# First-layer attention scores: one unit per head on two row halves of TensorE, instead of one unit per two batch rows on the whole array

## The reference, cut to what matters

```python
q = (q_in @ wq + bq).reshape(Bq, Sq, H, DK).transpose(0, 2, 1, 3)   # H = 16, DK = 64
k = (k_in @ wk + bk).reshape(...); v = (v_in @ wv + bv).reshape(...)
scores = einsum('bhqd,bhkd->bhqk', q, k)
scores = where(mask, scores, NEG_INF)          # causal in "sa", padding in both
attn = nan_to_num(softmax(scores / sqrt(DK), axis=-1))
out = einsum('bhqk,bhkd->bhqd', attn, v)...reshape(...) @ wo + bo
```

## Time and profile before

| what | value |
|---|---|
| median of three runs | 2354.99 us |
| the profiled execution | 2356.81 us |
| its span | 2355.1 us |
| granted TensorE clock, mean | 0.964 of full |
| PE busy | 2094.1 us (89%) |
| DVE busy | 1398.9 us (59%) |
| ACT busy | 1138.5 us (48%) |
| POOL busy | 243.7 us (10%) |
| DMA | 8 GB/s over the span |

### The profile page before, as it was taken

How to read it: one execution, slowest core, us unless ns; L and a number is a source line. 1 busy time by engine, 2 the same in 40 slices (tenths; PEclk the granted TensorE clock), 3 DMA queues, 4 the chain that set the end, 5 groups by cost and what they waited for, 6 DMA issues and landing times.

```text
span 2355.1 us, 34008 instructions
## 1 busy us (share of the span) xinstructions
PE 2094.1 (89%) x12584; PEld 1433.4 (61%) x12584; DVE 1398.9 (59%) x3674; ACT 1138.5 (48%) x3857; POOL 243.7 (10%) x271
## 2 busy tenths in 40 slices
PE   5877998899898988999898988999898988897799
PEld 2555666657665666656665666656665666654455
DVE  4544658666675658566675568567675668524410
ACT  3453736456362736456363736456463736331222
POOL 1001011010101011010101011010101011001100
PEclk9989999999999999999999899999999999989999
DMA  5000000000000000000000000000000000000001
GB/s 177 1 1 15 1 1 1 1 15 1 1 1 15 1 1 1 1 15 1 1 1 16 1 1 1 1 16 1 1 1 5 1 1 1 1 1 1 1 10 27
DMA packets 25129, 20.00 MB, mean 8 GB/s; under 512 B 2243, under 2 KB 22790, under 8 KB 24966
## 3 DMA queue, kind: packets, MB, share of 16 engines
q1 hardware_dynamic: 24966, 17.83, 2.6%
HBM read 15.73 MB, written 2.10 MB: 8 GB/s over the span
## 4 chain that ended last, share of the span: by engine, by line
PE 63%; DVE 21%; ACT 11%; issue 4%; POOL 1%; SPq 1%; DMA 0%; POOLq 0%; DVEq 0%
PE ps L655 15%; PE ps L663 9%; PE ps L700 7%; PE ps L798 5%; ACT s_probs L1032 4%; PE ps L785 3%; PE ps L640 3%; PE ps L651 3%; PE ps L813 3%; PE ps L725 3%; ACT probs L1032 3%; DVE keys L1278 3%; DVE stats L1198 2%; DVE probs L1234 2%; DVE tok L1211 2%
## 5 line engine op out<-in xcount | busy, mean ns | idle before, releaser
L1032 ACT ACTIVATE probs<-ps,neg_max 128x128 f32<-128x128 f32 x1024 | 364.9, 378 | 337.1 <-DVE neg_max L1191 336.9
L700 PE MATMUL ps<-keys,queries 128*128 128x256 f32 x1024 | 285.6, 404 | 25.9 <-ACT queries L1026 25.9
L1032 ACT ACTIVATE s_probs<-ps,s_max 128x128 f32<-128x128 f32 x768 | 209.1, 392 | 101.4 <-DVE s_max L1191 100.8
L1191 DVE TENSOR_REDUCE neg_max<-ps 128x4 f32<-128x512 f32 x256 | 176.4, 689 | 129.2 <-PE ps L703 128.0
L700 PEld LDWEIGHTS ps<-keys,queries 128*128 128x128 f32 x1024 | 185.2, 199 | 61.6 <-ACT queries L1026 33.0
L1032 ACT ACTIVATION_READ_ACCUMULATOR probs<-ps,neg_max 128x1 f32 x1024 | 220.6, 216 | 0.0
L1198 DVE BATCH_NORM_STATS2 stats<-ps 128x6 f32<-128x128 f32 x352 | 78.4, 286 | 236.6 <-PE ps L663 229.8
L546 POOL TENSOR_TENSOR rstd<-var_eps,minus_half 128x4 f32<-128x4 f32 x88 | 94.3, 1072 | 1153.3 <-DVE var_eps L1204 1153.3
L1026 ACT ACTIVATE probsT<-ps 128x512 f32<-128x512 f32 x256 | 158.3, 618 | 36.7 <-PE ps L711 35.2
L1191 DVE TENSOR_REDUCE s_max<-ps 128x4 f32<-128x512 f32 x192 | 123.7, 686 | 83.4 <-PE ps L785 82.9
L711 PE MATMUL ps<-ident,probs 128*128 128x128 f32 x1024 | 160.4, 280 | 6.0 <-DVE probs L1234 3.6
(11 more groups left out here) (208 smaller groups left out, 3723.1 us busy)
## 6 DMA issues: line engine op xcount, KB each, us to landing
x_in<-in_x SPq DMA_DIRECT2D x8, 256.0 KB, 3.6
c_in<-in_ctx SPq DMA_DIRECT2D x8, 256.0 KB, 3.8
skip_in<-in_mask_BxS_ik SPq DMA_DIRECT2D x8, 256.0 KB, 3.8
out<-headsT SPq DMA_DIRECT2D x28, 64.0 KB, 1.8
valid_in<-in_mask_BxS_bf SPq DMA_DIRECT2D x8, 64.0 KB, 3.5
w_qkv_sa<-in_L_xattn_sa_wq SPq DMA_DIRECT2D x1, 512.0 KB
w_qkv_sa<-in_L_xattn_sa_wk SPq DMA_DIRECT2D x1, 512.0 KB
w_qkv_sa<-in_L_xattn_sa_wv SPq DMA_DIRECT2D x1, 512.0 KB
```

Source lines behind the costliest of these rows:

```text
L700: mm(bank(MAIN, item)[:, n * 256:n * 256 + 256], queries[:, c % 2, at], keys[:, c % 2, :, at], start=(n == 0), stop=False, skip_group_chec ...
L1032: last = A(dst[:, u % dst.shape[1], h * 128:h * 128 + 128], bank(st, (tag, "s", u))[:, h * 128:h * 128 + 128], ACT.Exp, bias=src_max[:, u ...
L1191: V.tensor_reduce(dst[:, u % 2, :], bank(st, (tag, "s", u)).rearrange("p (h k) -> p h k", h=4), AX.X, ALU.max, negate=True).then_inc(max_r ...
```

## The change

`scores` works on a whole chunk when it comes to the even unit. Unit 2c is now head 0 of all four sequences, and unit 2c + 1 is head 1. TensorE first multiplies the mask into both banks (two 512-column bf16 matmuls), and then runs eight score matmuls of 128 columns that use 64 rows of the array each: rows 0 to 63 for head 0 into one bank, rows 64 to 127 for head 1 into the other, alternately. `keys` holds one version, so it is copied out by one instruction of 128 partitions, and the zeroing at the start goes. `main_steps` puts `s(s)` and `s(s+1)` into the even step; the other items keep their order. A step that held nothing but the odd `s` ("ca", s = 15) is no longer there, so that the list has 115 steps instead of 116. `scale_probs` now has two scalars per tile, and is four `tensor_scalar` instructions of 128 columns where it was two `scalar_tensor_tensor` of 256. `probs` has four slots instead of three. The diff, cut to its core:

```diff
@@ main_steps, attention
-            first = [(tag, "s", s)] if s < UNITS else []
+            first = [(tag, "s", s), (tag, "s", s + 1)] if s < UNITS and s % 2 == 0 else []
...
-        keys = sb("keys", [128, 2, 2, GT])
+        keys = sb("keys", [128, 2, GT])
...
-        probs = sb("probs", [128, 3, 512])
+        probs = sb("probs", [128, 4, 512])
...
-            link(P.memset(keys[64:128, :, 0, :], 0.0))
-            link(P.memset(keys[0:64, :, 1, :], 0.0))
@@ scores
-                c, b0 = u // 2, 2 * (u % 2)
-                before_filling(i, item, (tag, "k", c), (tag, "q", c))
-                for n in range(2):
-                    at = slice((b0 + n) * T, (b0 + n) * T + T)
-                    mm(bank(MAIN, item)[:, n * 256:n * 256 + 256], queries[:, c % 2, at], keys[:, c % 2, :, at],
-                       start=(n == 0), stop=False, skip_group_check=True)
-                mask = (mask_sa if tag == "sa" else mask_ca)[:, b0:b0 + 2, :]
-                mm(bank(MAIN, item), ident_h[:, :], mask.unsqueeze(2).broadcast_to([128, 2, 2, T]),
-                   start=False, stop=True, skip_group_check=True).then_inc(filled[MAIN], 1)
+                if u % 2:
+                    return
+                c = u // 2
+                before_filling(i, item)
+                before_filling(i, (tag, "s", u + 1), (tag, "k", c), (tag, "q", c))
+                mask = (mask_sa if tag == "sa" else mask_ca)[:, :, :]
+                for h in range(2):
+                    mm(bank(MAIN, (tag, "s", u + h)), ident_h[:, :], mask, start=True, stop=False, skip_group_check=True)
+                for b in range(G):
+                    for h in range(2):
+                        rows_of = slice(64 * h, 64 * h + 64)
+                        last = mm(bank(MAIN, (tag, "s", u + h))[:, b * T:b * T + T], queries[rows_of, c % 2, b * T:b * T + T],
+                                  keys[rows_of, c % 2, b * T:b * T + T], start=False, stop=(b == G - 1), skip_group_check=True)
+                        if b == G - 1:
+                            last.then_inc(filled[MAIN], 1)
@@ outputs: which probsT unit and columns
-                    u, n = 2 * c + b // 2, b % 2
                     for h in range(2):
+                        u = 2 * c + h
...
-                                  probsT[:, u % PT, (2 * n + h) * 128:(2 * n + h) * 128 + 128], start=True, stop=True)
+                                  probsT[:, u % PT, b * T:b * T + T], start=True, stop=True)
@@ ScalarE, kind "k" (VectorE likewise)
-                            for h in range(2):
-                                rows_of = slice(64 * h, 64 * h + 64)
-                                last = A(keys[rows_of, c % 2, h, :], bank(MAIN, item)[rows_of, :], ACT.Identity,
-                                         bias=cols[f"L0_xattn_{tag}_bk"][rows_of, c:c + 1], scale=1.0)
-                            last.then_inc(emptied[MAIN, "A"], 1)
+                            A(keys[:, c % 2, :], bank(MAIN, item), ACT.Identity,
+                              bias=cols[f"L0_xattn_{tag}_bk"][:, c:c + 1], scale=1.0).then_inc(emptied[MAIN, "A"], 1)
@@ scale_probs
-                for n in range(2):
-                    p = probs[:, u % 3, n * 256:n * 256 + 256].rearrange("p (h k) -> p h k", h=2)
-                    last = V.scalar_tensor_tensor(out=p, in0=p, scalar=row_ok[tag][:, b0 + n:b0 + n + 1],
-                                                  in1=inv[:, u % 3, 2 * n:2 * n + 2].unsqueeze(2).broadcast_to([128, 2, T]),
-                                                  op0=ALU.mult, op1=ALU.mult)
+                for b in range(G):
+                    p = probs[:, u % 4, b * T:b * T + T]
+                    last = V.tensor_scalar(p, p, inv[:, u % 3, b:b + 1], row_ok[tag][:, b:b + 1], ALU.mult, ALU.mult)
```

10 lines of the change are left out of this document (3 added, 7 removed).

## The result

The changed kernel takes 2446.83 us, median of four runs (2438.45 to 2451.42), beside 2353.64 for the kernel before on the same chip: ratio 1.0391, 95% interval 1.0369 to 1.0413, slower. The forecast was 2391, in a range of 2315 to 2440. The direction was right, the size was not: +93 us instead of +36.

What follows compares the result with a forecast made beforehand. PE, busy 89%, looked like the bound, but waits for ScalarE and VectorE would decide. Seven groups x (6.1 - 0.6) = 38.5 us, first group -3, gave +36: 2355 becomes 2391 us, range 2315 to 2440.

Steps and rivals of the forecast that it cites:

- Scores on PE: Score matmuls of a pair: halves run side by side, 2.15 to 1.70 us, gaining 58 us of PE work over 128 pairs.
- The forecast fall of PE's busy time by 50 us: Whole span, a sign to check: PE's busy time falls by some 50 us while its idle time grows by 85.
- Keys' copy: Copying keys out of PSUM: one instruction instead of two, ScalarE 1.37 to about 0.68 us, VectorE 2 x 0.75 to 0.75.
- Scaling: scale_probs on VectorE: four instructions take 1.3 us a unit against 0.9, 100 us more in all, mostly hidden.
- The ring in the first group: Pairs without side stream: 7.65 us becomes 8.5 (keys by ScalarE) or 6.65 (keys by VectorE), -3 us for the group.
- a sign of being wrong: First group against later groups: the forecast is wrong if the first group loses as much as the others.
- Cross-attention: Eight pairs beside L2: copies and normalised tiles come later behind both units' exponentials and maxima, +6.1 us a group.
- s = 2: Cross-attention pair where the block's layer norm comes later: 11.45 us against 9.0, +2.5.
- Self-attention: Eight pairs beside L1: PE's gain is given back to ScalarE's queue, -0.6 us a group.
- The rest of a group and the end: Layer norms, FFN and the end of each group keep their work: counted as nothing.
- Waits of PE, to grow for ScalarE and for the normalised tiles: PE's waits for keys, kx, s_probs and VectorE's normalised tiles grow, most in cross-attention.
- The clock: PE's granted clock: more standing can lower it, one hundredth costing up to 23 us; named for the range above 2391.

Runs made afterwards that it cites:

- e3: Kernel before with scaling as four tensor_scalar of 128 columns instead of two instructions of 256: 2371.84 us, ratio 1.0059.
- e5: Changed kernel plus six unused matmuls ahead of query projections of chunks 2, 4 and 6 (62 us of added PE work): 2429.85 us, ratio 1.0327.
- e1: Changed kernel, but VectorE and ScalarE take the second unit's maxima and exponentials at their old place, in the odd step: 2397.37 us, ratio 1.0182.
- e16: e11 measured again, unchanged: 2347.73 us, ratio 0.9979 to the kernel before.
- e9: e1 with each mask multiplied twice, 55 us of added PE work inside the scores: 2417.20 us, ratio 1.0210.
- e11: e1 with scaling as a 128x4 product and one product over 512 columns instead of four tensor_scalar: 2350.88 us, ratio 0.9919.
- e12: Changed kernel with scaling as a 128x4 product and one product over 512 columns instead of four tensor_scalar: 2434.20 us, ratio 1.0354.
- e10: Kernel before, whole array, with TensorE filling both units in the even step and maxima and exponentials left in place: 2442.47 us, ratio 1.0315.
- e19: Kernel before with the key projection ahead of the scores in the even step on all engines: 2382.21 us, ratio 1.0126.
- e21: Kernel before plus six unused matmuls ahead of query projections of chunks 2, 4 and 6 (62 us of PE work): 2401.62 us, ratio 1.0198.
- e7: Changed kernel, but ScalarE and VectorE handle the keys' copy between the two units' maxima and exponentials: 2448.28 us, ratio 1.0349.

## Why the prediction was wrong, step by step

- **Scores on PE, 2.15 to 1.70 us a pair.** Right, a little better: 1.61. The Trainium skill, "TensorEngine Tiling (Array Packing)", Key Properties, says that tiles work in parallel and that a change of tiling drains the engine; this trace agrees: the scores take 1.61 us where the halves one by one would have taken 2.17 and more, and the two masks take 0.52 where 2 x 0.215 would be 0.43, the same 0.09 as the forecast read off. The forecast fall of PE's busy time by 50 us didn't show (2094 to 2112 us), since the work ran at a lower clock; at full clock it is there. I had offered it as a test without seeing that. (The projection at 73.87 takes 1.12 us and not 1.13, which changes nothing.)
- **Keys' copy.** Right: 0.72 and 0.74 us.
- **Scaling, 1.3 us a unit.** Too high: 1.11 (four instructions of 0.34, 0.28 apart), so some 60 us more on VectorE and not 100. e3 prices it at 0.6% in the kernel before.
- **The ring in the first group.** Right at full clock for its pairs: 8.5 forecast and 8.54 (e5) for ScalarE's keys, 6.65 and 6.51 (67.25 - 60.74 in e5) for VectorE's. The group's gain of 3 us did not come: by span times clock it is there (205.29 x 0.96 = 197 against 192), but PE stood for 7 us more, and with the clock of 0.89 the group lost 10.6. It lost as much as the later groups, which the forecast had named as a sign of being wrong.
- **Cross-attention, +6.1 us a group.** Right: +6.5, at the same clock. For s = 2 the transposition of the normalised tile was forecast 5.85 us into the pair and the queries 7.35:

```profile
1204.77 0.59 PE L701 MATMUL ps<-mask_ca,ident_h 128*128 128x512 bf16 x2
1205.29 1.16 PE L705 MATMUL ps<-keys,queries 64*128 64x128 f32 x16
...
1210.24 0.66 PE L649 MATMUL ps<-ident,tok 128*128 128x128 f32 x4 [1.75 <-DVE tok L1212]
1211.88 1.84 PE L653 MATMUL ps<-xT_b,w_qkv_ca 128*128 128x512 f32 x2 [0.98 <-ACT keys L1059]
1213.51 1.91 PE L653 MATMUL ps<-x_side,w_sq 128*128 128x512 f32 x2
...
1218.13 1.16 PE L705 MATMUL ps<-keys,queries 64*128 64x128 f32 x16
```

  They came at 5.47 and 7.11 us. After these two waits the clock was at half for the next products (1.84 and 1.91 us instead of 1.1), and the pair took 1218.13 - 1205.29 = 12.84 us instead of 11.45. The order of the earlier trace rows was replayed rightly, and the level of the clock behind it not at all. That the sum of the eight pairs came within 0.4 us all the same is in part luck: this one is 1.4 us over, and others are as much under.
- **Self-attention, -0.6 us a group.** Wrong by 3.5 us in the group shown: +2.9, at 0.87 instead of 0.93.
- **The rest of a group and the end, at nothing.** Wrong: 10.6 - 6.5 - 2.9 = 1.2 us in a later group, and by the same count 9.5 us in the last group and behind it, where the clock is 0.93 instead of 0.96.
- **Waits of PE, to grow for ScalarE and for the normalised tiles.** Right for keys (16.3 to 42.2 us) and `kx` (6.1 to 26.8); wrong for `s_probs` (6.6 to 6.8) and for the normalised tiles (`tok`: 53.1 to 54.2), which hardly grew.
- **The clock.** This is the step that failed. The forecast said that more standing of PE can lower the granted clock and that a hundredth is up to 23 us, and then priced it at nothing in the sum and at two hundredths at most in the range. It fell by 2.8 hundredths. By span times clock that is up to 72 of the 94.6 us; by the strict division it is 67, and the mechanism that I had summed, less work and more waits, came to -50 + 77 = +27 and not +36. e1's two kinds of groups, e16 beside e1, and e5 show that this share is real. Some 70% of the loss hung on a sentence that entered no number.

The Trainium skill, "TensorE: Matmul & The Clock Gate", A second HAM failure mode: psum-queue depth-cycling, describes a kernel in which PE idles briefly between groups of matmuls, bank after bank, often enough for the clock to go down and up again. This trace agrees in the pattern: no wait for keys was longer than 2.80 us, and the time at half clock grew from 170 to 314 us. The prediction took from that page only what a load costs.

**Still open.** What the clock costs is shown; what brings it down is not. How the fall of 0.028 divides between more waits and thinner work isn't settled: e5 gives back 0.014 by filling some waits, e9 0.014 in e1 by thickening the work, and neither returns to 0.964. e1 and e16, with the same matmuls and nearly the same standing, differ by 0.023, so neither total decides it. Nor is it shown why one dose of work on VectorE (e11) moves e1's clock by two hundredths and the changed kernel's (e12) not at all; the last section has what the traces say of it. That the second unit's scores lost as cover make e10's 76 us was argued from the order; no run puts that cover back alone. What e10's trace shows is 49 us more standing of PE than before (310 against 261) and 32 us more lost to the clock.

## What to carry to other kernels

In a kernel whose TensorE is busy for nearly all of its time, price the clock as a term of its own, with a number: take the product of time and clock for the same group in several places of the trace, and ask what a hundredth costs (here some 25 us). A change that takes work from TensorE and makes its waits more and longer can pay twice, once for the wait and once for the slow work behind it. Such a change should be tried with the consumers of the new results left at their old places first: that alone was worth 40 to 50 us here, and beside the halves it came from shorter waits, not from the clock.

## What was not expected of the hardware

The groups of these kernels do not simply take the time that their work would suggest: most of their periods stand on a ladder. Four first row maxima of the changed kernel, one per group:

```profile
796.47 0.69 DVE L1192 TENSOR_REDUCE neg_max<-ps 128x4 f32<-128x512 f32 x1 [0.83 <-PE ps L705]
1069.55 0.69 DVE L1192 TENSOR_REDUCE neg_max<-ps 128x4 f32<-128x512 f32 x1 [0.82 <-PE ps L705]
1342.62 0.69 DVE L1192 TENSOR_REDUCE neg_max<-ps 128x4 f32<-128x512 f32 x1 [0.82 <-PE ps L705]
1615.69 0.69 DVE L1192 TENSOR_REDUCE neg_max<-ps 128x4 f32<-128x512 f32 x1 [0.82 <-PE ps L705]
```

They are 273.08, 273.07 and 273.07 us apart, and the half-clock stretches fall at the same places in each. Periods that come again are 259.4, 262.8, 266.1, 269.6, 273.1, 276.5, 279.9 and 283.3 us, 3.4 us from one to the next. Not all stand on this ladder: e9, e19 and e21 change between two periods from group to group, of which at least one lies off it (269.1 and 273.7, 265.3 and 267.1, 266.7 and 269.2), and e5 and e11 come to no rest. The changed kernel, e7, e10 and e12 all end at 273.1, though "full" differs by tens of microseconds over their runs; e1 goes from 263.0 to 269.6 in the middle of a run and stays. A kernel seems to settle into a period in which work and clock repeat together. If so, a small edit is often worth either nothing or a whole step, which over seven groups is 24 us; this would fit that the later groups of e12 and e7 end at the changed kernel's period, and that the same product was worth 50 us in e1. It is an observation from the traces, and no experiment was made on it.
